# A two-hop graph kernel on one core: a drain behind each single matmul and transpose in both hops, and one PSUM operand in the second hop's large VectorE products

## The reference

```python
a_input = jnp.concatenate([ent[head], ent[tail]], axis=-1)
e_input = jnp.sum((a_input @ fc_w.T + fc_b) * rel[etype], axis=-1)
e = jax.nn.leaky_relu(e_input, negative_slope=0.2)
m = jax.ops.segment_max(e, head, num_segments=n)
exp_e = jnp.exp(e - m[head])
alpha = exp_e / segment_sum(exp_e, head)[head]
ent = segment_sum(ent[tail] * alpha[:, None], head) + ent
...                                            # twice, with ent / norm(ent) behind each hop
return _layernorm(x + ent)
```

## Time and profile before

| | us |
|---|---|
| median of three runs (2864.08 to 2873.38) | 2866.54 |
| profiled execution | 2870.03 |
| its span | 2867.7 |
| first hop's stretch, 389 to 1604 | 1215 |
| second hop's stretch, 1684 to 2856 | 1172 |

### The profile page before, as it was taken

How to read it: one execution, slowest core, us unless ns; L and a number is a source line. 1 busy time by engine, 2 the same in 40 slices (tenths; PEclk the granted TensorE clock), 3 DMA queues, 4 the chain that set the end, 5 groups by cost and what they waited for, 6 DMA issues and landing times. The chain is left out here.

```text
span 2867.7 us, 22941 instructions
## 1 busy us (share of the span) xinstructions
PE 1218.3 (42%) x4597; PEld 818.2 (29%) x4597; DVE 1848.4 (64%) x3677; ACT 866.2 (30%) x1585; POOL 1805.7 (63%) x1607
## 2 busy tenths in 40 slices
PE   4688801354423544245433534444344345343300
PEld 4577701122211222123212423232223223222200
DVE  6867864286562865546655559877667667766753
ACT  2232304375453754445631212111111111111111
POOL 1000047377774777757777238877777787777776
PEclk9555555555555555555555556665655555566555
DMA  2333333254432444335433133222222222222210
GB/s 68 89 109 103 104 70 84 52 147 131 126 91 71 130 132 131 86 95 150 122 87 114 51 112 89 82 85 79 61 83 87 72 66 84 86 58 66 60 44 13
DMA packets 91815, 255.95 MB, mean 89 GB/s; under 512 B 31782, under 2 KB 39047, under 8 KB 91771
## 3 DMA queue, kind: packets, MB, share of 16 engines
q1 hardware_dynamic: 41403, 183.66, 20.8%
q0 software_dynamic: 50368, 71.78, 11.4%
HBM read 157.76 MB, written 102.23 MB: 91 GB/s over the span
## 5 line engine op out<-in xcount | busy, mean ns | idle before, releaser
L572 POOL DMA_INDIRECT area<-rows,gi x1176 | 1330.2, 1131 | 487.4 <-issue 367.7
L620 POOL DMA_INDIRECT out<-area,place x392 | 459.3, 1172 | 119.5 <-issue 119.5
L765 PE MATMUL psR<-area,row_t 128*98 128x512 f16 (+1 forms) x896 | 302.7, 504 | 454.3 <-DVE area L1191 335.9
L748 PE MATMUL psR<-area 128*128 128x392 f16 x392 | 198.5, 506 | 445.2 <-issue 406.3
L670 PE MATMUL psP<-V,vT 65*125 65x40 f32 (+1 forms) x1586 | 323.4, 393 | 86.1 <-issue 56.6
L670 PEld LDWEIGHTS psP<-V,vT 65*125 65x125 f32 (+1 forms) x1586 | 316.0, 310 | 104.7 <-issue 62.4
L765 PEld LDWEIGHTS psR<-area,row_t 128*98 128x98 f16 x896 | 141.5, 173 | 610.4 <-DVE area L1191 351.9
L908 ACT ACTIVATE area<-area 128x896 f32<-128x896 f32 x84 | 79.8, 950 | 586.2 <-DVE area L1270 433.6
L872 ACT ACTIVATE area<-iota_h,half_hi 128x392 f16<-128x392 f16 x392 | 238.9, 609 | 16.8 <-issue 15.4
L1269 DVE TENSOR_TENSOR area<-SM,rd 128x896 f32<-128x896 f32 x56 | 93.6, 1671 | 206.6 <-DMA out<-area,place 205.4
L774 PE MATMUL psT<-ones,area 98*128 98x1 f32 x700 | 152.6, 352 | 173.5 <-DVE area L1191 131.1
(11 more groups left out here) (269 smaller groups left out, 2296.4 us busy)
## 6 DMA issues: line engine op xcount, KB each, us to landing
rows<-area SPq DMA_DIRECT2D x50, 787.5 KB
area<-tail_digits SPq DMA_DIRECT2D x28, 896.0 KB
rows<-area SPq DMA_DIRECT2D x28, 735.0 KB
area<-rows SPq DMA_DIRECT2D x28, 735.0 KB
area<-rows SPq DMA_DIRECT2D x25, 787.5 KB
area<-rows,gi POOLq DMA_INDIRECT x1176
head_xs<-area SPq DMA_DIRECT2D x28, 448.0 KB
area<-head_xs SPq DMA_DIRECT2D x28, 448.0 KB
```

Of the source, the lines that this page charges most:

```text
L572: pool.indirect_dma_start(out=to[:, b, k, 0:tab.shape[1]], out_offset=None, in_=tab, in_offset=bass.IndirectOffsetOnAxis(ap=gi[:, b, n, k: ...
L620: pool.indirect_dma_start(out=out, out_offset=bass.IndirectOffsetOnAxis(ap=place[:, b, k:k + 1].bitcast(U32), axis=0), in_=rowO[:, b, k, 0 ...
L748: te.matmul(psC, sign_lo[:, (s0 + k) % KS, :], sign_hi[:, (s0 + k) % KS, :], start=static and t0 + k == 0, stop=True, skip_group_check=True)
L765: te.matmul(psR[g % 2][0:HH, 0:w], row_t[:, n, c, :], hot_lo[:, c, 4 * g * P:4 * g * P + w], start=c == 0 and n == 0, stop=c == HB - 1 and ...
```

## The change

It has two parts. On TensorE each matmul and transpose of the hops gets a drain of its own (an instruction that ends when what is before it on the engine has ended); the semaphore increment moves from an instruction of its own onto the last drain. The node products of the first 389 us keep one drain (`single=False`). By the built programs, the loop body of a pair of chunks has 42 drains before and 88 after in the first hop, and 10 before and 92 after in the second; no other instruction of TensorE is added or moved.

On VectorE and ScalarE, in the second hop alone, one input or the output of each large product is placed in PSUM banks that TensorE doesn't use at that time: `typ`, the score sum `fa`, `ex`, `decay`, `rd`, `rs`, `mean`, `part`, the numerator `held`, and copies of `iota_r`, `first_end`, `first_A` and `last_A`. The instructions and their order stay; five small ones (four copies and a memset) are added once, between the hops. Where `fa` was a strided view of `cap`, it is now contiguous.

```diff
+        flatT = psT[:, :, :].rearrange("p n x -> p (n x)")
+        held = flatT[:, 0:K * C].rearrange("p (k c) -> p k c", c=C)
+        held_A = flatT[:, 0:K * R].rearrange("p (k r) -> p k r", r=R)
+        held_typ = flatT[:, K * R:2 * K * R].rearrange("p (k r) -> p k r", r=R)
+        held_ex = psP[:, 1, 512 - 2 * K:512].rearrange("p (n k) -> p n k", n=2)
+        held_decay = psP[:, :, :].rearrange("p n x -> p (n x)")[:, 0:CO * (K + 1)].rearrange("p (c k) -> p c k", k=K + 1)
...
                         te.transpose(psT[0:w, t // KT, (k - t) * P:(k - t) * P + parts], row(k),
-                                            ident[0:parts, 0:parts])
-                    pe.drain()
-                    pe.sem_inc(tr, 1)
+                                     ident[0:parts, 0:parts])
+                        last = pe.drain()
+                    last.then_inc(tr, 1)
...
-            def products(n, parts, w, pr):
+            def products(n, parts, w, pr, single=True):
...
+                    if single or k == n - 1:
+                        last = pe.drain()
+                last.then_inc(pr, 1)
...
                             te.matmul(psR[g % 2][0:HH, 0:w], row_t[:, n, c, :], hot_lo[:, c, 4 * g * P:4 * g * P + w],
                                              start=c == 0 and n == 0, stop=c == HB - 1 and n == 1)
-                    pe.drain()
-                    pe.sem_inc(s_look, 1)
+                            last = pe.drain()
+                    last.then_inc(s_look, 1)
...
                     te.matmul(sums[:, k:k + 1], chosen[0:HH, k * P:(k + 1) * P], ones[0:HH, 0:1], start=True, stop=True)
-                pe.drain()
-                pe.sem_inc(s_sum, 1)
+                    last = pe.drain()
+                last.then_inc(s_sum, 1)
...
-                    sc_.activation(ex[:, :, :], dl[:, :, :], ACT.Exp).then_inc(s_exp, 1)
+                    ex_, decay_ = (ex[:, :, :], decay) if h == 0 else (held_ex, held_decay)
+                    sc_.activation(ex_, dl[:, :, :], ACT.Exp).then_inc(s_exp, 1)
...
-                link(ve.tensor_tensor(vv, agg, wide(rd[:, 0:K0], K0), ALU.mult))
-                ve.tensor_tensor(vv, vv, rowsH[:, :, 0:C], ALU.add).then_inc(s_sq, 1)
+                via, rd_, rs_, mean_ = (vv, rd, rs, mean) if h == 0 else (held[:, 0:K0, :], held_rd, held_rs, held_mean)
+                link(ve.tensor_tensor(via, agg, wide(rd_[:, 0:K0], K0), ALU.mult))
+                ve.tensor_tensor(vv, via, rowsH[:, :, 0:C], ALU.add).then_inc(s_sq, 1)
...
-                        fa, la = (cap[:, n * R:(n + 1) * R, :].rearrange("p r k -> p k r") for n in range(2))
+                        fa, la = held_A, cap[:, 0:R, :].rearrange("p r k -> p k r")
...
-                                          ex[:, 1:2, :].to_broadcast([P, CO, K]), ALU.mult))
-                    link(ve.tensor_tensor_scan(S[:, :, :].rearrange("p c k -> p (c k)"), decay[:, :, :].rearrange("p c k -> p (c k)"),
+                                          ex_[:, 1:2, :].to_broadcast([P, CO, K]), ALU.mult))
+                    link(ve.tensor_tensor_scan(S[:, :, :].rearrange("p c k -> p (c k)"), decay_[:, :, :].rearrange("p c k -> p (c k)"),
...
-                        fe = first_end[:, cc]
+                        fe = (first_end if h == 0 else held_end)[:, cc]
```

More of the change, by code:

```diff
@@ L689, in node_products @@
                     pe.wait_ge(s_nb, j)
-                products(KN, PN, 2 * R, s_npr)
+                products(KN, PN, 2 * R, s_npr, single=False)
             def node_half(n):
@@ L749, in count @@
                               start=static and t0 + k == 0, stop=True, skip_group_check=True)
-                    pe.drain()
-                    pe.sem_inc(s_cnt, 1)
+                    pe.drain().then_inc(s_cnt, 1)
             def look(j, sums):
@@ L1282, in finish @@
                 else:
[L1283 to L1284 removed]
+                    link(ve.tensor_tensor(via, vv, wide(rs_[:, 0:K0], K0), ALU.mult))
+                    link(ve.tensor_tensor(vv, via, rowsX, ALU.add))
                     free()
[L1287 to L1289 removed]
+                    link(ve.tensor_reduce(mean_[:, 0:K0], vv, AX.X, ALU.add))
+                    link(ve.tensor_scalar(mean_[:, 0:K0], mean_[:, 0:K0], 1.0 / C, None, ALU.mult))
+                    ve.tensor_tensor(vv, vv, wide(mean_[:, 0:K0], K0), ALU.subtract).then_inc(s_sq, 1)
                     meanwhile[1]()
@@ L1328, in chunk @@
                         hots(*look)
-                    link(ve.tensor_tensor(typ[:, :, :], iota_r[:, :].unsqueeze(1).to_broadcast([P, K, R]),
+                    typ_, iota_ = (typ, iota_r) if h == 0 else (held_typ, held_iota)
+                    ex_, decay_, rd_, part_ = (ex, decay, rd, part) if h == 0 else (held_ex, held_decay, held_rd, held_part)
+                    link(ve.tensor_tensor(typ_[:, :, :], iota_[:, :].unsqueeze(1).to_broadcast([P, K, R]),
                                           wide(type_f[:, cc], K, R), ALU.is_equal))
@@ L1370, in capture @@
                             keep_A(j - 2, b)
-                        fe = first_end[:, cc]
+                        fe = (first_end if h == 0 else held_end)[:, cc]
                         link(ve.tensor_tensor(cap[:, :, :], SM[:, :, 1:K + 1], fe.unsqueeze(1).to_broadcast([P, CO + 1, K]), ALU.mult))
-                        link(ve.tensor_reduce(part[:, :], cap[:, :, :], AX.X, ALU.add))
-                        link(ve.tensor_tensor(first[:, :], first[:, :], part[:, :], ALU.add))
+                        link(ve.tensor_reduce(part_[:, :], cap[:, :, :], AX.X, ALU.add))
+                        link(ve.tensor_tensor(first[:, :], first[:, :], part_[:, :], ALU.add))
                         if nodes:
@@ L1444, in _ @@
                 link(ve.tensor_scalar(first[:, C:CO], first[:, C:CO], 1e-30, None, ALU.max))
-                link(ve.reciprocal(rd[:, 0:1], first[:, C:CO]))
+                link(ve.reciprocal((rd if h == 0 else held_rd)[:, 0:1], first[:, C:CO]))
                 dve.wait_ge(s_sg, 16 + 32 * h)
```

39 lines of the change are left out of this document (22 added, 17 removed).

## The result

The changed kernel takes 3369.69 us (median of four runs, 3355.51 to 3435.25), the kernel before 2869.96 beside it: a ratio of 1.172, 95% interval 1.165 to 1.180. It is slower by 17% where 5% faster was forecast, and outside the forecast range. Some executions of any kernel here are a few per cent longer at the same work (3435.25 us is one), and every ratio in this document leaves them out on both sides.

The account below looks back on a forecast made before the run. GpSimd was taken to bound the second hop at 41.5 us per chunk; 2870.03 - 109 (second hop) - 60 (first hop) + 10 (seam) = 2711, forecast 2710 us, range 2630 to 2890 (own range 2660 to 2755).

Parts of the forecast that it names:

- GpSimd's floor of 36.4 us: Second hop: with gathers at 0.94 and scatters at 0.98 us unheld, GpSimd's chunk falls from 41.5 to 36.4 us.
- PSUM operands at no cost on VectorE: Second hop: reading PSUM costs nothing, writing 0 to 1.8 us per chunk, hidden in VectorE's slack.
- The drains' own price: Second hop, TensorE: matmuls with a drain each cost their duration plus a 0.21 us gap, 36.1 us per look against 18.8.
- the ring: Second hop: TensorE's groups and sums follow one another around VectorE's takings, closing at 36.8 us per chunk.
- Part 2, drains in the second hop: Priced TensorE's drained look at 36.8 us; with GpSimd and VectorE coupled, a 37.5 us period, -109 us over 27 periods.
- part 1: PSUM operands in the second hop: VectorE's large products stop holding GpSimd, -5.1 us per chunk.
- The cover: Second hop: the drains' extra 17 us per look lie in TensorE's idle time, its waits of 12.06 and 6.36 us.
- Rival 4: Late drains beside an unheld GpSimd become the bound: 5 of 46 per look at 2.1 us, 3046 us; chance 0.21.
- First hop, -60 forecast: First hop: drains behind at most two records end long stalls, saving 60 of up to 105 us of GpSimd's waits.
- Seam, +10 forecast (0 to +35): Between the hops: two looks' extra 17 us partly show, plus five small instructions, +10 us.

## Why the prediction was wrong

**GpSimd's floor of 36.4 us: right.** 960 and 986 ns; a run of 28 DMAs takes 35.3 to 37.0 us. The Trainium skill ("SBUF — State Buffer", section "Who interferes with whom") was right that products with one SBUF input don't hold GpSimd, and its other inference, that products never do, fell: 1184 ns against 960.

**PSUM operands at no cost on VectorE: right.** The division, which now writes PSUM, takes 1.67 us, as before, and the product with `rs` 1.10 for 1.12.

**The drains' own price: right in kind, too high.** 36.8 us was forecast for a look; with GpSimd paced it is 9.14 for the sums (10.9 forecast) and about 22 for the groups (25.2), and the ring fits under 42.5.

**The step that failed** is in "Part 2, drains in the second hop": it took TensorE's instructions at their quick pace and let the ring close at 36.8 us. That pace held in the kernel before because VectorE held GpSimd back to one DMA in 1.48 us, and part 1 takes just that away. The gain of part 1 is itself the cause of the larger loss: at 1.29 us per DMA the sums take 33 us instead of 8, and GpSimd then waits 20.6 us in the mean for the indices. The reading of the earlier trace rows was the error behind it: "a drain that notices late that the engine is empty, the later the more matmuls are before it". A burst's drain is late because the loads and matmuls before it come slowly, and the modelled ends in the trace draw them as done. Splitting the burst only spreads the same lateness over more drains. The cover failed with it: the prediction laid the drains' extra 17 us into TensorE's idle time, but behind late sums the look's groups are waited for.

**Rival 4** named the place and the cause (unheld GpSimd all of the time) with a chance of 0.21 and 3046 us. Its price was 2.1 us for each of 5 late drains, taken from a single-matmul row; measured, the sums alone are over 20 us per look late. Against it I had set the median of 392 single drains at 0.507 us; a median over a hop in which GpSimd is partly held or waiting says nothing of the stretches in which it isn't.

**First hop, -60 forecast, +42 measured.** The step that failed is the one that gave single drains 60 us of GpSimd's waits: drains cure no stall (the experiment with the bursts in the first hop). Pauses of GpSimd cure more than half of the long ones.

**Seam, +10 forecast (0 to +35), +60 measured.** There GpSimd is idle, TensorE is alone on the path, and three rounds of look, transposes and products follow one another. One round of before, and one of the changed kernel:

```profile
1624.90 5.36 PE L774 MATMUL psR<-ones,area 98*128 98x1 f32 x28 [1.39 <-DVE area L1191]
1630.49 4.24 PE L661 MATMUL psT<-ident,area 128*65 128x128 f32 x14 [0.23 <-issue]
1635.21 6.20 PE L670 MATMUL psP<-V,vT 65*128 65x40 f32 x28 [0.48 <-ACT vT L831]
1641.79 5.96 PE L765 MATMUL psR<-area,row_t 128*98 128x512 f16 x16 [0.38 <-issue]
1648.84 3.08 PE L765 MATMUL psR<-area,row_t 128*98 128x512 f16 x16 [1.09 <-DVE area L1191]
```

```profile
1690.31 9.14 PE L787 MATMUL psR<-ones,area 98*128 98x1 f32 x28 [0.62 <-DVE area L1205]
1699.68 7.63 PE L674 MATMUL psT<-ident,area 128*65 128x128 f32 x14 [0.23 <-issue]
1707.79 10.10 PE L683 MATMUL psP<-V,vT 65*128 65x40 f32 x28 [0.48 <-ACT vT L844]
1718.26 21.84 PE L778 MATMUL psR<-area,row_t 128*98 128x512 f16 x32 [0.38 <-issue]
```

A round grows from 28.4 us (1624.90 to the next sums at 1653.32) to 50.4 (1690.31 to 1740.73). I counted the looks' drains only, and partly; there is no cover at all. The sum had no term for TensorE's clock either: its share is 0.50 in the changed kernel's seam where it was 0.61, and the 32 matmuls of 512 columns that took 5.96 and 3.08 us take 21.84.

**What stays open:** where TensorE's instructions are held up. The runs show that GpSimd's issuing decides it; no row shows which resource the two share. It isn't TensorE's alone. The register instructions of VectorE's sequencer (ALU_OP) last 0.04 us in the median; in the second hop 43 of 913 of them last some 0.70 us in the changed kernel and 52 of 913 with PSUM operands alone, none sooner than 15 us into a run of GpSimd, and none of 935 in the kernel before nor of 913 in any kernel with pauses there (worked out from the traces). Whether GpSimd's mean pace decides or how long it issues without relief is open as well: the late stretch begins some 10 us into a run, which speaks for length, and no experiment holds the one still and moves the other. Nor does the table give a threshold: two other kernels with the second hop of before had sums of 13.3 and 14.1 us at the same 1.48.

## What to carry to other kernels

Before you take away a stall of an engine, ask who runs well only because of it: here the stall of GpSimd was the pause that TensorE's instructions needed, and giving GpSimd its full pace, with no drain added, took the second hop's chunk from 41.7 to 51.2 us. A drain that ends late in a trace is a reading of everything in front of it on its engine, not of the drain; test it by halving what is in front before you split the burst, and set its end beside what the other engines did until then: here it came some 4 us behind GpSimd's last DMA in most chunks, whatever was queued. Where software DMAs run back to back beside an engine with idle "issue" gaps, try a few short pauses on the issuing engine: here six in each chunk of the first hop made the kernel 2% faster, and with PSUM operands and pauses in the second hop 3%.

## What the runs showed of the hardware

- Beside indirect DMAs issued each 1.29 us in the mean, 28 in a run, the sums of a look (28 matmuls and 28 loads) take 33 us; with six pauses of 1.1 us among them (1.52 us in the mean), 6.1 us. In the changed kernel the slow stretch begins 9.4 to 13.3 us into such a run and ends 2.9 to 4.0 us behind it. The Trainium skill ("SBUF — State Buffer", section "Who interferes with whom") says that PE never waits on anyone; for its ports no run speaks against that, for its instructions these do.
- With a drain behind every matmul TensorE stayed at its lower clock (1.2 GHz): the granted clock is 0.50 in all three stretches after the change, where it was 0.51, 0.61 and 0.59, and 0.50 too in the second hop with pauses; 16 matmuls of 512 columns take 11.74 us with drains against 5.30 without. In the seam of before, 16 matmuls of groups 2 and 3 took 3.08 us; with drains a whole look of 32 takes 21.84.
